# Low-rank rows taken out of the values' products, query copies behind the exponentials, and a moved start of the finishing work

## The chip, the cores and the metric

The kernel runs on one core of one Trainium2 chip. The metric is device time in microseconds for one launch; before the change, three runs took 1050.96, 1053.4 and 1054.88 us, median 1053.4. Times in the trace come from one further, profiled execution.

The engines are named as in the profile: PE multiplies matrices (PEld is its weight load, which overlaps), DVE, ACT and POOL work on vectors, SP only issues DMAs. Each engine runs its own instructions strictly in the order in which they were written, and waits at semaphores for the others. Work is accumulated in PSUM and copied from there to SBUF by ACT and DVE.

## The reference

All is in float32. The batch has 8 sequences of 256 rows of 1,024 features.

```
h    = x @ W.T + b + 2 * (x @ A[slot]) @ B[slot]     # rank 16, one slot per sequence
q, k, v = h @ w_q, h @ w_k, h @ w_v                  # 32 heads, 8 key/value heads, 32 wide
o    = softmax(q k^T / sqrt(32)) v                   # 4 query heads share a k/v head
x1   = x + o @ w_o
c    = x1 @ weight[id].T                             # one 1024x1024 matrix per sequence
out  = x1 + sum_e gate_e(c) * 4 * (c @ A_e.T) @ B_e.T   # 4 experts of rank 16, top 2 by a router
```

The kernel never forms h. It multiplies W and w_q, w_k, w_v once (the fold), so that q, k and v are x times folded weights plus a rank-16 part: u = 2 x A, then u times B folded in the same way. The rank-16 part of all of q, k and v uses the same u. The expert rows A_e and the router's rows are likewise multiplied into each sequence's matrix ("conditioned rows", 68 of them).

Each product of two float32 matrices is made from three products of rounded parts: high x high, high x low, low x high. So a value on its way to PE is first copied as its high part (mostly by ACT), then its low part is the difference (mostly by DVE).

## The kernel before

**Fold stage.** 192 tiles of folded weights are made in three rounds of 4 column blocks (`CHUNKS`), 8 tiles each. Between rounds ACT and DVE copy the folded bias-like rows (`bp`, `brow`), and split the next round's weights (`split_q`, 8 pieces a round).

**Attend stage.** The sequences go in 4 pairs; a pair has 8 key/value heads x 2 sequences = 16 steps (`STEPS`), together N = 64. In step n PE does, in this order (`step` in `tensor`, L838): scores of step n for the maxima, first two of four tiles (L801); work part 0; the outputs of step n-3 (L825, L829); the transposition ("turn") of step n-1's maxima (L836); transposed scores of step n-2, two of four (L812); the other two score tiles of step n; work part 1; the last two transposed scores of n-2. ACT makes the exponentials of the transposed scores (L600), DVE the maxima (L673) and their split into high and low (L679, L681), POOL sums the exponentials (L550), SP sends the maxima to the rows of `q_stack` where they are subtracted by the matmul itself.

**Work** is the projections. The table `WORK` lists for each of a pair's 16 steps what its two parts hold: a unit such as q5 (128 columns of queries for 2 sequences, 24 matmuls of 512 columns and one of the rank-16 part) may be cut, q5:0-3 are the first 3 of its 8 k-steps. A "+" is a unit of the next pair. `SEQ` is the order of units. Unit `u` (L740, L742) makes the rank-16 rows u for both sequences, from the hi and lo parts of A in `a_stack`; v0 to v3 (L774, L776) make the values of 128 tokens each, with 256 columns. The unit's result lies in one of two PSUM banks (`bank`), in turn: the first matmul of a unit waits (`free`, L719) until the unit two before it has been read by ACT (`proj_act`) and by DVE (`proj_dve`).

**Who reads a unit when** is set by `evacuated` (L321): ACT copies units of part 0 before the second pair of exponentials of the same step, those of part 1 behind all exponentials. For q and k, ACT makes 4 copies (L566) and DVE takes 4 differences (L653), then SP issues a DMA that doubles the high part (L479) and PE may use it only then. The next pair's x lands in 8 pieces, ACT copies its high parts (L428: 6 pieces at the end of step 11, 2 at the end of 12), DVE its low parts (L432: steps 12 and 13).

**Finish stage.** Per sequence: `load_o` brings the attention's outputs and the reciprocals of the sums (5 DMAs, L946), `normalise` multiplies them (L1013, DVE), `scale_hi` and `scale_lo` split them; 8 output tiles with w_o (L1043, 24 matmuls of 256 columns each), added to x (`residual`); 8 conditioned rows (L1071), for which POOL loads a 512 KB piece each and ACT and DVE split it (L1052, L1056); then the experts. Part of it is placed in the last pair's steps, whose table of work has holes where a next pair's units would be: `WO_LOAD`, `WO_SPLIT`, `FIRST_TILES` (the 8 output tiles of the first sequence, the first in part 1 of step 12 behind q7, the last in part 0 of step 16), `ROWS_SPLIT` and `ROWS_MULT` (splits and matmuls of the first conditioned rows). Steps are counted from the last pair's start. Rows 5 to 7 come in `first()`, behind the attend stage.

## Time and profile before

| | |
|---|---|
| median of 3 runs (range) | 1053.4 us (1050.96 to 1054.88) |
| the profiled execution | 1050.6 us, of which the span of the trace is 1048.9 us |
| PE busy | 1013.4 us, 97% of the span, 6,934 matmuls |
| weight loads busy | 820.2 us, 78% |
| DVE busy | 633.5 us, 60% |
| ACT busy | 449.5 us, 43% |
| POOL busy | 234.0 us, 22% |
| chain of waits that ended last | PE 90%, DMA 3%, DVE 3% |
| DMA | 117.4 MB, mean 112 GB/s |
| granted TensorE clock, mean | 0.988 of full speed |

"Busy" is the time in which an engine executes; a busy PE may still run at the lower clock. The chain of waits goes back from the last instruction, at each step to what released it. The rows on which the prediction rests stand in a section of their own below; "[1.06 <-PE psS L801]" behind a row of a timeline means that the engine stood idle for so long ahead of it, and what ended that.

### The profile page before, as it was taken

To read this page: it belongs to the slowest core of one execution; us is meant where nothing else is said; L and a number is where in the kernel's file an instruction comes from. 1 tells how busy PE (TensorE), PEld (TensorE's weight loads), DVE (VectorE), ACT (ScalarE), POOL (GpSimd) and SP (SyncE) were. 2 spreads that over 40 slices of the span, in tenths; PEclk is the share of its full clock that TensorE was granted. 3 is DMA by queue.
4 is the path that set the end of the run, shared out by engine and by line. 5 is a ranking of instruction groups with operands and counts; after the bars stand their busy time and mean duration, and the time that the engine had idled before them with its cause. 6 is when DMAs were issued, how large, how long until landed. Compare 5 with 4: busy or idle time off the path is not lost.

```text
span 1048.9 us, 17421 instructions
## 1 busy us (share of the span) xinstructions
PE 1013.4 (97%) x6934; PEld 820.2 (78%) x6934; DVE 633.5 (60%) x1071; ACT 449.5 (43%) x782; POOL 234.0 (22%) x224
## 2 busy tenths in 40 slices
PE   7999999999999999999999999999899999999997
PEld 6878787877678776787767787676589998988986
DVE  6562724667856578664776657654665655655653
ACT  5121223355754557554665556635422332323321
POOL 1000001123323233223332246643111111111100
PEclk9999999999999999999999999999999999999998
DMA  7030312111421124211232134453966756766531
GB/s 263 0 101 1 131 47 73 27 38 43 123 55 38 29 56 122 60 40 27 53 113 60 42 93 142 123 154 142 257 215 197 229 193 199 228 196 205 201 122 40
DMA packets 49888, 117.41 MB, mean 112 GB/s; under 512 B 7298, under 2 KB 26114, under 8 KB 45712
## 3 DMA queue, kind: packets, MB, share of 16 engines
q1 hardware_dynamic: 40080, 81.70, 26.4%
q0 software_dynamic: 9728, 34.61, 10.4%
q8 instruction: 55, 0.90, 0.4%
q14 instruction: 25, 0.20, 0.1%
HBM read 86.38 MB, written 18.89 MB: 100 GB/s over the span
## 4 chain that ended last, share of the span: by engine, by line
PE 90%; DMA 3%; DVE 3%; ACT 1%; SPq 1%; issue 1%; POOL 0%; ACTq 0%
PE psP L759 20%; PE psW L1043 17%; PE psF L254 11%; PE psG L1071 8%; PE psO L825 6%; PE psT L812 5%; PE psS L801 5%; PE psP L774 4%; PE psX L1286 3%; PE psO L829 2%; PE psY L1305 2%; PE psF L265 1%; DMA x_raw<-in_xT 1%; PE psM L836 1%; PE psP L740 1%; PE psP L742 1%
## 5 line engine op out<-in xcount | busy, mean ns | idle before, releaser
L673 DVE TENSOR_REDUCE nmax<-psS 128x2 f32<-128x512 f32 x256 | 164.5, 684 | 153.8 <-PE psS L801 152.1
L550 POOL TENSOR_TENSOR p_sum<-probs 128x512 f32<-128x512 f32 x128 | 167.6, 1310 | 372.6 <-ACT probs L600 372.3
L759 PE MATMUL psP<-x_hl,wq 128*128 128x512 f32 x960 | 235.1, 392 | 0.6 <-DVE q_stack L653 0.6
L759 PEld LDWEIGHTS psP<-x_hl,wq 128*128 128x128 f32 x960 | 175.2, 189 | 32.8 <-issue 0.8
L1043 PE MATMUL psW<-wq 128*128 128x256 f32 x1536 | 196.7, 283 | 1.6 <-DVE q_stack L653 1.2
L1043 PEld LDWEIGHTS psW<-wq 128*128 128x128 f32 x1536 | 190.3, 191 | 6.2 <-issue 1.3
L600 ACT ACTIVATE probs<-psT 128x512 f32<-128x512 f32 x256 | 139.2, 596 | 54.4 <-PE psT L812 53.9
L1052 ACT ACTIVATE cond_hi<-cond_raw 128x1024 fp32r<-128x1024 f32 x64 | 66.8, 1057 | 152.5 <-PE psG L1071 148.1
L1056 DVE TENSOR_TENSOR cond_lo<-cond_raw,cond_hi 128x1024 fp32r<-128x1024 f32 x64 | 78.3, 1235 | 89.1 <-ACT cond_hi L1052 89.0
L812 PE MATMUL psT<-q_stack,k_stack 98*128 98x512 f32 x256 | 90.1, 427 | 7.7 <-ACT probs L600 5.4
L653 DVE TENSOR_TENSOR q_stack<-psP,q_stack 32x512 fp32r<-32x512 f32 x128 | 87.8, 686 | 9.2 <-ACT q_stack L566 7.1
L801 PEld LDWEIGHTS psS<-k_stack,q_stack 96*128 96x128 f32 x512 | 80.0, 190 | 12.7 <-DVE nmax L673 1.1
L615 ACT ACTIVATE nmax_rows<-psM 16x128 f32<-16x128 f32 x64 | 17.1, 267 | 169.6 <-PE psM L836 169.6
L1003 POOL DMA_DIRECT2D cond_raw<-in_cond x64 | 33.8, 529 | 250.0 <-PE psG L1071 249.9
L801 PE MATMUL psS<-k_stack,q_stack 96*128 96x256 f32 x512 | 85.3, 287 | 0.1
L566 ACT ACTIVATE q_stack<-psP 32x512 fp32r<-32x512 f32 x128 | 75.2, 587 | 9.7 <-PE psP L766 8.1
L254 PE MATMUL psF<-q_hi,w_hi 128*128 128x512 f32 x184 | 72.0, 391 | 2.6 <-DVE bp L217 2.6
L254 PE MATMUL psF<-q_lo,w_hi 128*128 128x512 f32 x184 | 71.7, 389 | 0.0
L254 PE MATMUL psF<-q_hi,w_lo 128*128 128x512 f32 x184 | 71.6, 389 | 0.0
L825 PE MATMUL psO<-probs,v_sb 128*32 128x256 f32 x1024 | 69.3, 388 | 0.0
L812 PEld LDWEIGHTS psT<-q_stack,k_stack 98*128 98x128 f32 x256 | 43.0, 191 | 17.1 <-ACT probs L600 10.7
L825 PEld LDWEIGHTS psO<-probs,v_sb 128*32 128x32 f32 x1024 | 26.9, 110 | 31.5 <-issue 18.1
(122 smaller groups left out, 1252.8 us busy)
## 6 DMA issues: line engine op xcount, KB each, us to landing
cond_raw<-in_cond POOLq DMA_DIRECT2D x64, 512.0 KB, 4.1
x_raw<-in_xT SPq DMA_DIRECT2D x32, 256.0 KB, 3.9
q_stack<-q_stack SPq DMA_DIRECT2D x32, 256.0 KB, 3.1
o_scratch<-o_sb SPq DMA_DIRECT2D x64, 128.0 KB
o_raw<-rden_scratch SPq DMA_DIRECT2D x32, 256.0 KB, 5.4
o_raw<-o_scratch SPq DMA_DIRECT2D x8, 1024.0 KB, 8.8
...
outT<-x_sb SPq DMA_DIRECT2D x32, 256.0 KB, 2.5
```

Of the source, the lines that this page charges most:

```text
L254: mm = pe.matmul(psF[:, bank(j, m)], w[:, k, m * P:(m + 1) * P], q[:, k], start=(k == 0 and i == 0), stop=(k == KT - 1 and i == 2))
L550: pool.tensor_tensor(p_sum[:, heads], probs[:, 0, heads], probs[:, 1, heads], ALU.add).then_inc(sum_done, 1)
L600: nc.scalar.activation(probs[:, i % 2, (i // 2) * 512:(i // 2 + 1) * 512], psT[:, i % 2], ACT.Exp, scale=ATT_SCALE).then_inc(exp_done, 1)
L653: ins = dve.tensor_tensor(to(h), both(psP[32 * h:32 * h + 32, bank(p, u)]), f(hi(h)), ALU.subtract)
L673: dve.tensor_reduce(nmax[:, n % 2, 2 * hp:2 * hp + 2, qt], psS[:, i % 2].rearrange("p (h k) -> p h k", h=2), AX.X, ALU.max, negate=True).t ...
L759: mm = pe.matmul(out, wq[:, i, w, k * P:(k + 1) * P], x[:, k, part], start=(k == 0 and n_ == 0), stop=False)
L801: mm = pe.matmul(psS[:, i % 2, j * T:(j + 1) * T], q_stack[0:96, slot, c, 2 * hp + j, qt * P:(qt + 1) * P], k_stack[0:96, c, g], start=Tru ...
L812: pe.matmul(psT[:, kt], k_stack[0:98, c, g, kt * P:(kt + 1) * P], q_stack[0:98, slot, c, 2 * hp:2 * hp + 2].rearrange("p h t -> p (h t)"), ...
L825: pe.matmul(psO[HD * h:HD * h + HD, 0], v_sb[:, c, kt, g], probs[:, kt, h * T:(h + 1) * T], start=(kt == 0), stop=(kt == KK - 1))
L1043: mm = pe.matmul(out, wq[:, k, w, m * P:(m + 1) * P], o_part(n % 2, o)[:, k], start=(k == 0 and i == 0), stop=(k == KT - 1 and i == 2))
L1056: dve.tensor_tensor(cond_lo[:, r % RAW], cond_raw[:, r % RAW], f(cond_hi[:, r % SPLIT]), ALU.subtract).then_inc(cond_lo_done, 1)
L1071: mm = pe.matmul(psG[0:EC, half], a[:, k], w[:, half * 512:(half + 1) * 512], start=(k == 0 and i == 0), stop=(k == KT - 1 and i == 2))
```

## The change

1. Unit `u` and `a_stack` go. The low-rank factor A is put beside the folded weights of the values, in `v_hi`, so that the values' matmuls give 288, 272 and 256 columns instead of three times 256, and the additional columns are x A for the unit's 128 tokens. DVE sums its two parts (`u_tok`), a new unit `t` turns it by 4 PE transposes, and ACT and DVE write `u_stack`.
2. Values get their rank-16 part in two units of their own, r0 and r1 (2 matmuls each), which DVE adds to `v_sb`; `v_sb` exists twice, for alternate pairs.
3. The order of units is new (`SEQ`, `WORK`): v0 to v3, t, k0, q0, q1 of the next pair in the steps 13 to 15.
4. `evacuated` is replaced by `soon` (values, t, q0) and `late` (other q and k): their copies stand behind all exponentials of the step.
5. The splits of x are spread over steps 11, 12 and 13. In the fold stage `bp` and `brow` are copied behind 2 of the 8 splits.
6. The last pair: q7 ends in step 11; `load_o(0)` is issued at the end of step -1 (the step before the last pair's first), `normalise(0)` at the end of step 0; 7 output tiles come in steps 12 to 15, the eighth in `first()` between rows 5 and 6; conditioned rows start at step 16; splits of rows are spread; the second sequence's outputs are loaded and normalised in steps 13 to 16.

```diff
-    (["+u:0-4"], ["+u:4-8"]),
-    (["+k0"], ["+q0"]),
-    (["+q1:0-4"], ["+q1:4-8"]),
+    (["+v0:0-4", "+v1:0-4"], ["+v0:4-8", "+v1:4-8"]),
+    (["+v2", "+v3"], ["+t", "+k0"]),
+    (["+q0"], ["+q1"]),
...
-SEQ = ["u", "k0", "q0", "q1", "v0", "q2", "v1", "v2", "v3", "q3", "k1", "q4", "q5", "q6", "q7"]
...
+SEQ = ["v0", "v1", "v2", "v3", "t", "k0", "q0", "q1", "q2", "r0", "r1", "q3", "k1", "q4", "q5", "q6", "q7"]
...
-def evacuated(n, part):
-
-    if part:
-        return finished(n, 1)
-    late = [(p, u) for p, u in finished(n - 1, 0) if u == "v0"] if n else []
-    return late + [(p, u) for p, u in finished(n, 0) if u != "v0"]
...
+def soon(n, part):
+
+    return [(p, u) for p, u in finished(n, part) if u[0] not in "qk" or u == "q0"]
...
+def late(n):
+
+    return [v for part in range(2) for v in finished(n, part) if v not in soon(n, part)]
...
-            ins = nc.scalar.activation(a_stack[:, c, :, c * R:(c + 1) * R], a_raw[:, c], ACT.Copy)
+            ins = nc.scalar.activation(v_hi[:, :, factor(c, 0)], a_raw[:, c], ACT.Copy)
...
-            for unit_ in evacuated(n, 1):
+            for unit_ in late(n):
...
+        def copy_t(p):
+
+            act.wait_ge(proj_done, unit(p, "t") + 1)
+            nc.scalar.activation(u_stack[0:32], psP[0:32, bank(p, "t")], ACT.Copy, scale=LORA_SCALE)
+            nc.scalar.activation(u_stack[32:64], psP[0:32, bank(p, "t")], ACT.Copy, scale=LORA_SCALE).then_inc(proj_act, 1)
...
+            if p >= 2:
+                act.wait_ge(pv_done, STEPS * (p - 1))
+            nc.scalar.activation(v_sb[p % 2][:, c, t % 2],
+                                 psP[:, bank(p, f"v{t}"), c * V0:c * V0 + NKV].rearrange("p (g d) -> p g d", g=G),
                                  ACT.Copy).then_inc(proj_act, 1)
...
-            for unit_ in evacuated(n, 0):
+            for unit_ in soon(n, 0) + soon(n, 1):
...
+            if more and s == 12:
+                for k in range(3, 6):
+                    split_x_hi(act, p + 1, k)
...
-            if more:
-                for k in {11: range(0, 6), 12: range(6, KT)}.get(s, ()):
+            if more and s == 11:
+                for k in range(3):
                     split_x_hi(act, p + 1, k)
-            for unit_ in evacuated(n, 1):
-                if unit_[1][0] != "v":
-                    evacuate(*unit_)
+            for unit_ in late(n):
+                evacuate(*unit_)
...
+            if more and s == 12:
+                for k in range(6, KT):
+                    split_x_hi(act, p + 1, k)
...
+            if u[0] == "v":
+
+                c, rows = j // 2, NKV * (1 - j // 2)
+                dve.wait_ge(proj_done, unit(p, u) + 1)
+                if p and j == 0:
+                    dve.wait_ge(proj_done, unit(p - 1, "t") + 1)
+                dve.tensor_reduce(u_tok[:, j, c], psP[:, bank(p, u), rows:rows + 2 * R].rearrange("p (h r) -> p r h", h=2),
...
+            elif u[0] == "r":
+                values = v_sb[p % 2][:, j].rearrange("p k g d -> p (k g d)")
+                dve.wait_ge(proj_done, unit(p, u) + 1)
+                dve.wait_ge(proj_act, read_unit(p, f"v{2 * j + 1}") + 1)
+                dve.tensor_tensor(values, values, psP[:, bank(p, u)], ALU.add).then_inc(r_added, 1)
...
-                for k in {12: range(0, 6), 13: range(6, KT)}.get(s, ()):
+                for k in {12: range(3), 13: range(3, 6)}.get(s, ()):
                     split_x_lo(dve, p + 1, k)
-            for unit_ in evacuated(n - 1, 1) if n else [(0, "q1")]:
-                if unit_[1] != "u":
+            for unit_ in late(n - 1) if n else [(0, "q1")]:
+                evacuate(*unit_)
+            if more and s == 13:
+                for k in range(6, KT):
+                    split_x_lo(dve, p + 1, k)
+            for unit_ in soon(n, 0):
+                if unit_[1] != "q0":
                     evacuate(*unit_)
             ahead.vector(dve, n, 0)
...
                 q, v = i // NS, SEQ[i % NS]
-                if v in SEQ_DVE:
-                    pe.wait_ge(proj_dve, dve_unit(q, v) + 1)
+                if v[0] == "r":
+                    pe.wait_ge(r_added, 2 * q + int(v[1]) + 1)
+                else:
+                    pe.wait_ge(proj_act, read_unit(q, v) + 1)
+                    pe.wait_ge(proj_dve, read_unit(q, v) + 1)
...
+        def turn_rows(p):
+            free(p, "t")
+            pe.wait_ge(proj_dve, read_unit(p, "v3") + 1)
+            for t in range(TILES):
+                mm = pe.transpose(psP[0:32, bank(p, "t"), t * P:(t + 1) * P],
+                                  u_tok[:, t].rearrange("p c r -> p (c r)"), id_sb[:])
+            mm.then_inc(proj_done, 1)
...
+        def project_v(p, t, first, end):
+
+            c, toks = t // 2, slice(t * P, (t + 1) * P)
+            if first == 0:
+                free(p, f"v{t}")
+                if t == 0:
+                    pe.wait_ge(a_lo_done, p + 1)
+            out = psP[:, bank(p, f"v{t}")]
+            hi_rows, lo_rows, lo_out = ((slice(V0, VC), slice(V0, VC - R), slice(0, NKV + R)) if c == 0 else
+                                        (slice(0, VC - V0), slice(R, VC - V0), slice(R, NKV + V0)))
+            for k in range(first, end):
+                if t == 0:
+                    pe.wait_ge(x_lo_done, KT * p + k + 1)
+                pe.matmul(out[:, 0:NKV + V0], x[:, k, 0, toks], v_hi[:, k, hi_rows], start=(k == 0), stop=False,
+                          skip_group_check=True)
+                pe.matmul(out[:, lo_out], x[:, k, 1, toks], v_hi[:, k, lo_rows], start=False, stop=False,
...
+                mm = pe.matmul(out[:, c * V0:c * V0 + NKV], x[:, k, 0, toks], v_lo[:, k], start=False, stop=(k == KT - 1),
...
+        def low_rank_v(p, c):
+            free(p, f"r{c}")
+            for t in range(2):
+                toks = slice(c * T + t * P, c * T + (t + 1) * P)
+                mm = pe.matmul(psP[:, bank(p, f"r{c}"), t * NKV:(t + 1) * NKV], u_stack[:, toks],
+                               b_stack[:, VB * P:(VB + 2) * P], start=True, stop=True)
+            mm.then_inc(proj_done, 1)
...
+    ROWS_HI = {14: [0], 15: [1], 16: [2, 3], 17: [4], 18: [5]}
+    ROWS_LO = {(15, 0): [0], (15, 1): [1], (16, 1): [2, 3], (17, 1): [4], (18, 1): [5]}
+    ROWS_MULT = {(16, 0): 0, (16, 1): 1, (17, 1): 2, (18, 0): 3, (18, 1): 4}
+    ROWS_LOAD = {13: range(4), 16: range(4, 6)}
...
-    FIRST_TILES = {(12 + (m + 1) // 2, (m + 1) % 2): m for m in range(KT)}
+    FIRST_TILES = {place: m for m, place in enumerate([(12, 0), (12, 1), (13, 0), (13, 1), (14, 0), (14, 1), (15, 0)])}
...
+        if s == -1:
+
+            sp.wait_ge(before.proj_done, unit(PAIRS - 1, "v3") + 1)
...
         if s == 13:
+            load_o(sp, 1)
             load_x(sp, 1)
-            load_o(sp, 1)
...
-        if s == 10:
+        if s == 1:
             scale_hi(act, 0)
...
+        if s == 15:
+            scale_hi(act, 1)
 
...
-        if part == 0 and s == 10:
+        if part == 1 and s == 0:
             normalise(dve, 0)
-        if part == 1 and s == 11:
+        if part == 1 and s == 2:
             scale_lo(dve, 0)
         m = FIRST_TILES.get((s, 0) if part else (s - 1, 1))
...
-        if part == 1:
-            for r in ROWS_SPLIT.get(s, ()):
-                cond_row_lo(dve, r)
+        if part == 1 and s == 14:
+            normalise(dve, 1)
+        for r in ROWS_LO.get((s, part), ()):
+            cond_row_lo(dve, r)
+        if part == 0 and s == 16:
+            scale_lo(dve, 1)
...
             pool.wait_ge(before.proj_done, PAIRS * NS)
-            load_cond(pool, 0, range(RAW))
+        if s in ROWS_LOAD:
+            load_cond(pool, 0, ROWS_LOAD[s])
...
                     cond_row(KT * n + m + 2)
+                if m == 5 and n == 0:
+                    residual(dve, 0, KT - 1)
...
-            for k in (5, 6, 7):
-                cond_row(pe, 0, k)
+            cond_row(pe, 0, 5)
+            w_o_tile(pe, 0, KT - 1, range(KT))
+            cond_row(pe, 0, 6)
+            cond_row(pe, 0, 7)
...
-            if j:
...
+            if j == 1:
+                act.wait_ge(bp_stored, 32)
...
+            if j + 1 < CHUNKS:
+                for k in range(2, KT):
+                    split_q(j + 1, k)
```

**PE at the start of a pair's step 13.** `psP` are the projections' banks. Before, behind the scores:

```order
L801 MATMUL psS<-k_stack,q_stack 128x256 [waits s_max]
L801 MATMUL psS<-k_stack,q_stack 128x256
L740 MATMUL psP<-x_hl,a_stack 64x256 [waits a_lo_done,x_lo_done,proj_dve,proj_act]
L742 MATMUL psP<-x_hl,a_stack 32x256
L740 MATMUL psP<-x_hl,a_stack 64x256
L742 MATMUL psP<-x_hl,a_stack 32x256
L740 MATMUL psP<-x_hl,a_stack 64x256 [waits x_lo_done]
```

In the change, at the same place; the third row from the end is the first matmul of v1, whose bank was q7's:

```order
L835 MATMUL psP<-v_hi,x_hl 128x272
L837 MATMUL psP<-v_lo,x_hl 128x256
L833 MATMUL psP<-v_hi,x_hl 128x288 [waits x_lo_done]
L835 MATMUL psP<-v_hi,x_hl 128x272
L837 MATMUL psP<-v_lo,x_hl 128x256
L833 MATMUL psP<-v_hi,x_hl 128x288 [waits x_lo_done]
L835 MATMUL psP<-v_hi,x_hl 128x272
L837 MATMUL psP<-v_lo,x_hl 128x256
L833 MATMUL psP<-v_hi,x_hl 128x288 [waits proj_dve,proj_act]
L835 MATMUL psP<-v_hi,x_hl 128x272
L837 MATMUL psP<-v_lo,x_hl 128x256
```

The 32 narrow matmuls of `u` are gone, and two units of the values are started in one part of the step, so a second wait for `proj_dve` and `proj_act`, that of the unit two before v1, now stands 12 matmuls behind the first.

**ACT in the steps 11 and 12 of a pair.** L428 and L566 of before are L471 and L606 of the change: pieces of the next pair's x, and the query copies. Before, from x piece 5 on:

```order
L428 ACTIVATE x_hl<-x_raw 128x512 [waits x_landed5]
L615 ACTIVATE nmax_rows<-psM 16x128 [waits turned]
L600 ACTIVATE probs<-psT 128x512 [waits pv_done,st_done]
L600 ACTIVATE probs<-psT 128x512 [waits st_done]
L608 ACTIVATE o_sb_83<-psO 128x512 [waits o_stored1,pv_done]
L566 ACTIVATE q_stack<-psP 32x2x256 [waits proj_done,st_done]
L566 ACTIVATE q_stack<-psP 32x2x256 x3
L600 ACTIVATE probs<-psT 128x512 [waits st_done] x2
L428 ACTIVATE x_hl<-x_raw 128x512 [waits x_landed6]
```

In the change, from x piece 2 on:

```order
L471 ACTIVATE x_hl<-x_raw 128x512 [waits x_landed2]
L656 ACTIVATE nmax_rows<-psM 16x128 [waits turned]
L641 ACTIVATE probs<-psT 128x512 [waits pv_done,st_done]
L641 ACTIVATE probs<-psT 128x512 [waits st_done]
L649 ACTIVATE o_sb_86<-psO 128x512 [waits o_stored1,pv_done]
L471 ACTIVATE x_hl<-x_raw 128x512 [waits x_landed3]
L471 ACTIVATE x_hl<-x_raw 128x512 [waits x_landed4]
L471 ACTIVATE x_hl<-x_raw 128x512 [waits x_landed5]
L641 ACTIVATE probs<-psT 128x512 [waits st_done] x2
L606 ACTIVATE q_stack<-psP 32x2x256 [waits proj_done,st_done]
L606 ACTIVATE q_stack<-psP 32x2x256 x3
```

The query copies (here q7's) have moved from ahead of the last two exponentials to behind them, and three pieces of x from ahead of the turned maxima (`nmax_rows`) to behind the output copy.

**DVE around the first normalisation.** L1013 of before is L1094 of the change; `nmax` are maxima. Before, in step 10 of the last pair:

```order
L679 CAST nmax_parts<-nmax 128x8 [waits s_max]
L681 TENSOR_TENSOR nmax_parts<-nmax,nmax_parts 128x8 [waits nmax_hi]
L673 TENSOR_REDUCE nmax<-psS 128x2 [waits s_done] x2
L1013 TENSOR_TENSOR o_raw<-o_raw 128x2048 [waits o_landed_0]
L673 TENSOR_REDUCE nmax<-psS 128x2 [waits s_done] x2
L679 CAST nmax_parts<-nmax 128x8 [waits s_max]
L681 TENSOR_TENSOR nmax_parts<-nmax,nmax_parts 128x8 [waits nmax_hi]
```

In the change, from step 0 of the last pair to step 1; L717 is the addition of r0 to the values:

```order
L733 CAST nmax_parts<-nmax 128x8 [waits s_max]
L735 TENSOR_TENSOR nmax_parts<-nmax,nmax_parts 128x8 [waits nmax_hi]
L1094 TENSOR_TENSOR o_raw<-o_raw 128x2048 [waits o_landed_0]
L727 TENSOR_REDUCE nmax<-psS 128x2 [waits s_done] x2
L717 TENSOR_TENSOR v_sb_83<-v_sb_83,psP 128x512 [waits proj_act,proj_done]
L727 TENSOR_REDUCE nmax<-psS 128x2 [waits s_done] x2
L733 CAST nmax_parts<-nmax 128x8 [waits s_max]
L735 TENSOR_TENSOR nmax_parts<-nmax,nmax_parts 128x8 [waits nmax_hi]
```

The wait for `o_landed_0` stands ten steps earlier, ahead of step 1's maxima and of r0's addition.

## Rows read from the trace of the kernel before

**Rows 1.** The page's first part: busy us, share of the span, instructions
```profile
PE 1013.4 (97%) x6934; PEld 820.2 (78%) x6934; DVE 633.5 (60%) x1071; ACT 449.5 (43%) x782; POOL 234.0 (22%) x224
```

**Rows 2.** What PE waited for: line and releaser, us, times, longest
```profile
PE psG L1071 <- DVE cond_lo L1056: 6.6, 4, 3.4
PE psT L812 <- ACT probs L600: 5.4, 3, 2.3
...
PE psF L254 <- DVE bp L217: 2.6, 2, 1.4
PE psT L812 <- DMA q_stack<-nmax_rows: 2.3, 1, 2.3
PE psW L1043 <- DVE q_stack L653: 1.2, 1, 1.2
```

**Rows 3.** Timeline, PE, the first pair's low-rank rows: start, length, line, operation, tiles
```profile
162.49 0.33 PE L740 MATMUL psP<-x_hl,a_stack 128*64 128x256 f32 x1
...
166.28 5.64 PE L759 MATMUL psP<-x_hl,wq 128*128 128x512 f32 x24
```

**Rows 4.** Timeline of PE, step 0 of the second pair
```profile
312.59 0.63 PE L801 MATMUL psS<-k_stack,q_stack 96*128 96x256 f32 x4
313.06 3.02 PE L774 MATMUL psP<-wq,x_hl 128*128 128x256 f32 x24
315.92 0.28 PE L776 MATMUL psP<-b_stack,u_stack 98*128 98x256 f32 x1
...
317.57 0.28 PE L836 MATMUL psM<-id_sb,nmax_parts 128*16 128x128 f32 x1
...
318.62 2.91 PE L759 MATMUL psP<-x_hl,wq 128*128 128x512 f32 x12
321.37 0.63 PE L812 MATMUL psT<-q_stack,k_stack 98*128 98x512 f32 x2
```

**Rows 5.** Timeline of ACT, the same step
```profile
312.56 1.09 ACT L600 ACTIVATE probs<-psT 128x512 f32<-128x512 f32 x2 [2.35 <-PE psT L812]
313.53 2.40 ACT L566 ACTIVATE q_stack<-psP 32x512 fp32r<-32x512 f32 x4
...
318.12 1.09 ACT L600 ACTIVATE probs<-psT 128x512 f32<-128x512 f32 x2
319.09 0.60 ACT L608 ACTIVATE o_sb<-psO 128x512 f32<-128x512 f32 x1
```

**Rows 6.** Timeline of DVE, the same step
```profile
318.58 1.29 DVE L673 TENSOR_REDUCE nmax<-psS 128x2 f32<-128x512 f32 x2 [1.06 <-PE psS L801]
...
320.64 0.17 DVE L681 TENSOR_TENSOR nmax_parts<-nmax,nmax_parts 128x8 fp32r<-128x8 f32 x1
```

**Rows 7.** Timeline of SP's DMA issues, the same step
```profile
315.95 0.56 SPq L479 DMA_DIRECT2D q_stack<-q_stack  x1
```

**Rows 8.** The page's sixth part: DMA issues, KB each, median us to landing
```profile
q_stack<-q_stack SPq DMA_DIRECT2D x32, 256.0 KB, 3.1
```

**Rows 9.** Groups of ACT's instructions: busy us, mean ns, idle before, releaser
```profile
L428 ACT ACTIVATE x_hl<-x_raw 128x512 fp32r<-128x512 f32 x32 | 19.8, 635 | 38.7 <-DMA x_raw<-in_xT 38.3
...
L587 ACT ACTIVATE v_sb<-psP 128x256 f32<-128x256 f32 x16 | 6.3, 395 | 8.1 <-PE psP L776 8.1
```

**Rows 10.** Groups of DVE's instructions, the same columns
```profile
L653 DVE TENSOR_TENSOR q_stack<-psP,q_stack 32x512 fp32r<-32x512 f32 x128 | 87.8, 686 | 9.2 <-ACT q_stack L566 7.1
```

**Rows 11.** Timeline of PE, before the second pair's low-rank rows
```profile
278.50 0.98 PE L812 MATMUL psT<-q_stack,k_stack 98*128 98x512 f32 x2 [1.39 <-ACT probs L600]
```

**Rows 12.** Timeline of SP's DMA issues, the first load of attention outputs
```profile
659.62 1.73 SPq L946 DMA_DIRECT2D o_raw<-rden_scratch  x4
```

**Rows 13.** Timeline of DVE, the first normalisation
```profile
669.52 2.29 DVE L1013 TENSOR_TENSOR o_raw<-o_raw 128x2048 f32<-128x2048 f32 x1 [4.35 <-DMA o_raw<-o_scratch]
```

**Rows 14.** Stretches: us, PE, PEld, DVE, ACT, POOL busy, PE clock, DMA share, GB/s
```profile
719.22:757.12 37.90, 30.21 (x218) 19.93 (x217) 20.79 (x28) 20.90 (x27) 10.63 (x13) 0.95 0.57 164
280.60:283.90 3.30, 3.30 (x22) 2.42 (x24) 3.23 (x5) 3.21 (x6) 1.01 (x1) 0.51 0.42 79
```

296 lines of the change are left out of this document (143 added, 153 removed).

## The prediction

> **What bounds the kernel now.** I read the busy shares first: PE is busy for 97% of the span [rows 1], so a matmul that goes comes off the span, and an idle PE is as dear as a matmul. The list of what PE waited for comes next [rows 2]; together it is small, and these entries bear on the change: 6.6 us for conditioned rows, 5.4 us for exponentials in three places, 2.6 us for `bp`, 2.3 us for an `nmax_rows` transfer, 1.2 us for a query's low part. The timelines of PE, ACT and DVE around one step [rows 4 to 6] then give a clock by which I place every moved instruction. Call T the start of a step's first scores (312.59), and "turn" its transposition of the maxima (317.57). Then: work begins at T+0.47; from the end of the first piece of work (about 316.04) to the turn are 1.53 us; the second piece of work begins at turn+1.05 [rows 4]. ACT does two exponentials until turn+1.64 and the output copy until turn+2.12; the exponentials at a step's end reach T+1.06 of the next, and four query copies behind them T+3.34 [rows 5]. DVE starts the second pair of maxima at turn+1.01 and has split them at turn+3.25 [rows 6].
>
> **Matmuls.** A pair's low-rank rows took 32 matmuls in 3.79 us [rows 3]; four pairs, one of them slowed in part by the clock: 14.9 us go. The value products widen from 3 x 256 columns to 288, 272 and 256. 24 of 256 columns take 2.86 us, 119 ns each, and 12 of 512 take 2.75, 229 ns each [rows 4], so 0.43 ns a column: 48 columns x 32 x 4 pairs = 2.6 us. Below, the widening could be free, if it is the weight load that sets the pace at 256 columns; above, if 288 and 272 cost as much as 512, 256 matmuls x 110 ns = 28 us. I take 2.4, next to the 256-column row. Sixteen transposes of 128 columns are new: between 0.03 us (gap behind the turn) and 0.12 us (a 256-column matmul) each, I take 1.2 in all. Low-rank matmuls for the values stay four a pair. Sum -11.3.
>
> **Fold.** `bp` and `brow` are copied behind two splits of queries' weights, not eight; PE's two waits, 2.6 us [rows 2], end, and the six splits moved behind have 11 us until PE wants them (k=2 comes two rounds of 24 matmuls later). -2.6. The first transposition waits for the fourth value unit's reduction, +0.6; a 0.6 us wait for q1 goes. Zero.
>
> **The pair's end, where x is split.** Before, ACT stood on a landing x and the exponentials came late, once in each of three pairs: 1.39 us in the first [rows 11], 5.4 us in all [rows 2]. Three of the splits now stand behind the output copy, so that goes: -5.4. What is late next is `v1`. Its PSUM bank was q7's, and q7 is now read last. ACT in step 12: until turn+2.12 as above, three x splits of 0.635 [rows 9] to 4.0, two exponentials (1.1) to 5.1, four copies (2.4) to 7.5. DVE: split maxima 3.25, two maxima of step 13 to 4.55, three x parts of 0.69 to 6.6, four lows of q7 of 0.686 [rows 10] to 9.35. PE reaches `v0` at turn+2.55, would start `v1` at 4.1, stops at `v0`'s fourth k until 5.2, and then at `v1` until 9.35. That is 5.2 us, in three pairs +15.6. Bounds: 3.4 each if ACT's copies alone counted (7.5), 6.6 if a late x holds ACT by the 1.4 us of before once more. Behind the standing `v1` are the outputs, the turn and the next exponentials, so nothing fills the gap.
> The transposition `t` in step 14 needs v2 copied, which ACT does behind exponentials and output copy: turn+2.12 and a copy of 0.395 [rows 9], 2.5; PE is there at turn+1.05. 1.5 us, three times: +4.5 (0 to 2 each).
>
> **Copies of queries behind exponentials.** They end at T+3.34; the duplicating DMA is issued at once [rows 7] and lands 3.1 us later [rows 8]: T+6.45 of the step after. q5 (needed after step 9 of 4 k-steps, 0.47+2.06+1.53+2.1 = 6.15) 0.3 us x 4; q6 (step 11, nothing in its second part, 6.0) 0.45 us x 3; q0, now finished in the pair's last step: ready at turn+2.12+2.4+3.1 = 7.6, wanted at turn+1.05+5.7+0.47 = 7.2, 0.45 us x 3. Together +4.0 (0 to 9). SP issues the next x loads behind q6's duplicate; x has 6 us of slack there.
>
> **The last pair.** `load_o(0)` moves to the end of step -1 and its normalisation to DVE at the end of step 0. SP issues it behind q1's duplicate: T+3.95. Before, five DMAs of 2.1 MB needed from 659.62 [rows 12] to 669.52, where DVE had waited 4.35 us [rows 13]: 9.9 us. So they land at T+13.9, the product of 2.29 ends at 16.2, the next maximum at 16.9, while PE wants that buffer at T+12.0 (6.9 for the step, 5.1 into the next). Behind DVE's wait stand maxima and r0's sum, for which q3 waits. 4.9 + 0.9 = 5.8 us against 2.3 before [rows 2]: +3.5. Bounds 0 and 9.
> The trace moved these loads at 212 GB/s. The Trainium skill, DMA: Bandwidth & Descriptors, section Specifications, gives some 358 GB/s for a core's share of HBM; by that the loads take 5.9 us, an estimate from the page, the wait shrinks to about 1 us and the whole sum would be some 5 us less. The measured landing decides.
> q7 is read before the first output tiles: -1.2 [rows 2], and 0.5 of small waits.
> Tail: the stretch 719.22 to 757.12 held 37.9 us with PE busy 30.2, in part at half clock [rows 14]. Rows 0 to 4 and their splits come half a step to a step sooner and a 2.9 us tile stands between rows 5 and 6, where the transfers of rows 6 and 7 are awaited. Against that row 0 now waits for the last maxima (about 1.0, behind a 2.29 normalisation on DVE) and the outputs for exponentials that ACT does late (1.6); 0.9 and 0.4 for rows 4 and 5, 2 of small ones: 27.5 of work + 5.9 = 33.4. -4.5 (-8 to +2).
>
> **Clock.** After the 1.39 us wait the granted clock was 0.51 of full, the lower level (1.2 GHz), for 3.3 us [rows 14]; at full load that costs 1.7 us. The waits that go had such stretches, and those that come will have them: three, the one for o, and perhaps one more than before. +1.7 (-5 to +7).
>
> **Sum.** -11.3 - 2.6 - 5.4 + 15.6 + 4.5 + 4.0 + 3.5 - 1.7 - 4.5 + 1.7 = +3.8. The profiled execution took 1050.6 us in all (span 1048.9, 1.7 around it); its like after the change 1054.4. The median of the runs is 2.8 above the profiled one, so 1057.2. I say 1057.
>
> **Rivals.** A, the forecast: new waits eat the matmuls saved, 1049 to 1059. For it: every one of them is an order on a strict queue. Its weakness: they are differences of long sums.
> B, slower by more than 0.5%: the clock. If PE falls to the lower level behind both pieces of the v1 wait and behind `t` as well, three pairs pay 2 x 1.7 more instead of one stretch in all: 6 x 1.7 - 1.7 = 8.5, giving 1065. It decides from a wait of about 1.4 us, which was enough in [rows 11, 14]. With only half of that, 1061. Against it: the rows show one stretch behind one wait, not two within 5 us.
> C, faster: the v1 wait is no longer than what it replaces, because DVE is free when q7's copies come (3.4 us each: 15.6 becomes 10.2), the duplicates land in time (4.0 goes) and so one clock stretch less: 1057 - 5.4 - 4.0 - 1.7 = 1046; with the o loads hidden as well (3.5), 1042. For it: DVE is busy only 60% [rows 1]; against it: not in these steps.
> D, the matmuls saved come through and nothing waits anew: 1053.4 - 11.3 - 2.6 - 5.4 - 4.5 - some of the clock = about 1027. That needs the bank wait of v1 not to be there, and the order of instructions shows it. Inside C's chance, 3 in 100.
> E, the widened products run at the 512-column price: +25, 1082; 2 in 100, inside B.
>
> **How the numbers follow.** A 0.42, B 0.35, C 0.23. Within 0.5% (5.3 us, about what these runs can tell from no change) is 1048.1 to 1058.7: almost all of A. Faster 0.23, same 0.42, slower 0.35. The range of 8 in 10 takes most of B and C: 1041 to 1067; A's own is 1049 to 1059.
>
> **What would show it.** PE busy some 10 us lower, and no `a_stack` matmul. Waits of PE: psP for DVE `q_stack` about 11 us in three places and for `x_hl` about 4; psP for ACT `v_sb` 4.5 us; psS for DMA `q_stack` a few tenths ten times; one stretch of 5 us at the last pair's second step with DVE's normalisation waiting for `o_raw`; `bp` gone. Wrong if the first of these is under 3 us in all (then C), or if the half-clock stretches are eight or more (then B).

## The result and the profile after

The changed kernel takes 1057.3 us (median of 18 runs, 1055.3 to 1060.4), the kernel before on the same chips 1053.5 us (18 runs, 1049.4 to 1057.0). The ratio is 1.0042, 95% interval 1.0028 to 1.0055: slower by 4.4 us by the ratio (the medians themselves are just under 4 us apart). A second measurement of the same file gave 1.0034 (1.0016 to 1.0052). The forecast said 1057, within 0.5% of the kernel before. One execution of c3, of 1403 us, and one of the kernel before beside it, of 2535 us, lie far outside all others and are left out below.

The profiled execution took 1060.4 us (span 1058.5). That is 3.1 us above the median of its kernel, where that of before lay 2.8 us below: the two spans differ by 9.6 us, the kernels by 4.4. What follows places the 9.6 us; the difference to 4.4 is taken up under the clock, below.

The first part of the page of the changed kernel answers to [rows 1]:

```profile
PE 1009.6 (95%) x6822; PEld 813.0 (77%) x6822; DVE 645.9 (61%) x1099; ACT 447.2 (42%) x786; POOL 236.8 (22%) x224
```

PE is busy 3.8 us less and idle 13.4 us more. What it waits for (line, releaser, us in total, times, longest), against [rows 2]:

```profile
PE psP L833 <- DVE q_stack L696: 13.6, 3, 4.5
...
PE psS L878 <- DVE nmax L727: 5.0, 5, 3.2
PE psP L795 <- ACT v_sb L627: 3.7, 3, 1.2
...
PE psP L833 <- DVE x_hl L475: 3.2, 3, 1.1
PE psT L889 <- DMA q_stack<-nmax_rows: 2.2, 1, 2.2
...
PE psG L1152 <- DVE cond_lo L1137: 1.3, 2, 0.9
PE psS L878 <- issue: 1.2, 4, 0.3
PE psO L902 <- ACT probs L641: 0.9, 1, 0.9
...
PE psS L878 <- DMA q_stack<-q_stack: 0.3, 1, 0.3
```

The waits for `bp`, those of the transposed scores for probabilities and most of those for `cond_lo` are gone; 13.6 us for q7's lows in three places are new, with 3.2 us for x. The first of these places in the timeline of PE (L833 and L837 are matmuls of the values, psO the outputs):

```profile
276.89 0.40 PE L833 MATMUL psP<-v_hi,x_hl 128*128 128x288 f32 x1 [1.07 <-DVE x_hl L475]
...
282.07 0.58 PE L833 MATMUL psP<-v_hi,x_hl 128*128 128x288 f32 x1 [4.54 <-DVE q_stack L696]
...
285.06 1.94 PE L902 MATMUL psO<-probs,v_sb 128*32 128x256 f32 x16
...
287.78 0.28 PE L913 MATMUL psM<-id_sb,nmax_parts 128*16 128x128 f32 x1
```

ACT in the same stretch, whose copies of q7 (L606) stand behind the exponentials:

```profile
276.32 2.38 ACT L606 ACTIVATE q_stack<-psP 32x512 fp32r<-32x512 f32 x4
278.61 1.13 ACT L471 ACTIVATE x_hl<-x_raw 128x512 fp32r<-128x512 f32 x2
288.10 0.27 ACT L656 ACTIVATE nmax_rows<-psM 16x128 f32<-16x128 f32 x1 [8.35 <-PE psM L913]
```

DVE in the same stretch, L475 being low parts of x, L696 q7's lows:

```profile
276.15 2.96 DVE L475 TENSOR_TENSOR x_hl<-x_raw,x_hl 128x512 fp32r<-128x512 f32 x3
279.14 2.79 DVE L696 TENSOR_TENSOR q_stack<-psP,q_stack 32x512 fp32r<-32x512 f32 x4
```

DVE makes three low parts of x, then q7's four lows until 281.9; 0.1 us later PE starts v1. Outputs, turn and exponentials follow late and at half clock (16 matmuls of the outputs take 1.94 us), so that ACT stands for 8.35 us.

The last pair's step 1, timeline of PE:

```profile
613.98 0.28 PE L913 MATMUL psM<-id_sb,nmax_parts 128*16 128x128 f32 x1
616.45 0.73 PE L889 MATMUL psT<-q_stack,k_stack 98*128 98x512 f32 x2 [2.20 <-DMA q_stack<-nmax_rows]
620.39 1.40 PE L878 MATMUL psS<-k_stack,q_stack 96*128 96x256 f32 x4 [3.20 <-DVE nmax L727]
621.59 2.93 PE L811 MATMUL psP<-x_hl,wq 128*128 128x512 f32 x6
```

DVE's normalisation (L1094) and the maxima behind it:

```profile
617.44 2.29 DVE L1094 TENSOR_TENSOR o_raw<-o_raw 128x2048 f32<-128x2048 f32 x1 [7.66 <-DMA o_raw<-o_scratch]
619.65 1.28 DVE L727 TENSOR_REDUCE nmax<-psS 128x2 f32<-128x512 f32 x2
```

SP issued the loads at 606.06, and the next maxima's transfer (`nmax_rows`) behind them in its queue:

```profile
606.06 2.01 SPq L1026 DMA_DIRECT2D o_raw<-rden_scratch  x4
...
608.58 1.36 SPq L536 DMA_DIRECT2D q_stack<-nmax_rows  x2
```

The granted clock was at the lower level, 1.2 GHz, in five stretches inside the kernel, as before, but each was 6.8 us long instead of 3.4. A further stretch stands at the very end in both traces, with PE busy 4.5 us in it before and 4.8 after, and is left out here. Windows laid on them in the trace of the changed kernel (us, busy time of PE, PEld, DVE, ACT, POOL, clock, DMA share, GB/s); the last follows no wait of the change:

```profile
280.70:287.50 6.80, 5.42 (x36) 3.77 (x36) 2.51 (x4) 0.00 (x0) 0.00 (x0) 0.52 0.02 5
420.70:427.50 6.80, 5.90 (x38) 3.96 (x39) 2.04 (x4) 0.00 (x0) 0.00 (x0) 0.52 0.00 0
557.20:564.00 6.80, 3.04 (x16) 2.83 (x20) 4.84 (x8) 1.43 (x3) 0.00 (x0) 0.52 0.19 41
618.60:625.40 6.80, 5.01 (x14) 4.08 (x15) 4.47 (x8) 0.42 (x1) 2.25 (x1) 0.52 0.06 21
762.00:768.80 6.80, 6.80 (x30) 5.72 (x30) 3.75 (x22) 1.27 (x2) 0.53 (x1) 0.52 0.80 218
```

The same on the five stretches of the kernel before:

```profile
280.50:283.90 3.40, 3.40 (x23) 2.52 (x24) 3.30 (x6) 3.31 (x6) 1.01 (x1) 0.53 0.41 77
413.70:417.10 3.40, 3.40 (x15) 3.10 (x16) 3.27 (x7) 3.33 (x7) 1.26 (x1) 0.51 0.01 2
550.20:553.60 3.40, 3.40 (x20) 2.59 (x22) 3.30 (x6) 3.34 (x7) 0.89 (x1) 0.52 0.40 77
669.60:673.00 3.40, 3.40 (x12) 2.87 (x11) 3.40 (x3) 3.20 (x6) 2.02 (x1) 0.53 0.00 0
734.50:737.90 3.40, 2.85 (x10) 1.34 (x14) 0.49 (x1) 0.00 (x0) 0.99 (x2) 0.52 0.79 239
```

PE worked 26.2 us at the lower level after the change (5.42 + 5.90 + 3.04 + 5.01 + 6.80) and 16.5 us before; half of the difference, 4.9 us, is its cost, an estimate from these windows.

The same places in both traces, from the timelines of PE, give this table:

| from, to | before | after | difference |
|---|---|---|---|
| start to the first product of the attend stage | 162.5 | 159.0 | -3.5 |
| to the turn in step 12 of the first pair (the x splits) | 113.4 | 112.8 | -0.6 |
| to the same turn of the second pair | 134.4 | 139.5 | +5.1 |
| to the same of the third | 134.5 | 139.4 | +4.9 |
| to the turn in step 2 of the last pair | 58.4 | 78.8 | +20.4 |
| to the turn in step 11 of the last pair | 75.3 | 63.0 | -12.3 |
| to the first transposed conditioned rows | 73.8 | 65.9 | -7.9 |
| to the end | 296.7 | 300.1 | +3.4 |

Much of the last pair's +20.4 and -12.3 is work that was moved: values and conditioned projections come early in the changed order. The middle rows are the plain ones: a whole pair's period is 5 us longer.

### The profile page after: what moved, and what is told of

The parts are those of the page before. It is cut to its first block, busy times and chain, and to the rows that moved or that the text cites. A ratio compares the mean times of both kernels' runs of the same rounds, so it can differ in the third digit from the quotient of the medians.

```text
span 1058.5 us, 17257 instructions
## 1 busy us (share of the span) xinstructions
PE 1009.6 (95%) x6822; PEld 813.0 (77%) x6822; DVE 645.9 (61%) x1099; ACT 447.2 (42%) x786; POOL 236.8 (22%) x224
## 4 chain that ended last, share of the span: by engine, by line
PE 88%; DVE 5%; DMA 3%; ACT 2%; issue 1%; POOL 1%; SPq 0%; ACTq 0%
PE psP L811 19%; PE psW L1124 16%; PE psF L280 12%; PE psG L1152 8%; PE psO L902 6%; PE psS L878 5%; PE psT L889 5%; PE psX L1375 3%; PE psO L906 3%; PE psP L833 2%; PE psY L1394 2%; PE psF L291 2%; DVE nmax L727 2%; PE psP L835 1%; PE psP L837 1%; DVE q_stack L696 1%
## 5 line engine op out<-in xcount | busy, mean ns | idle before, releaser
L592 POOL TENSOR_TENSOR p_sum<-probs 128x512 f32<-128x512 f32 x128 | 171.1, 1338 | 374.7 <-ACT probs L641 374.5
L811 PE MATMUL psP<-x_hl,wq 128*128 128x512 f32 x960 | 240.2, 393 | 0.2 <-DVE v_sb L717 0.2
L1133 ACT ACTIVATE cond_hi<-cond_raw 128x1024 fp32r<-128x1024 f32 x64 | 66.9, 1057 | 151.5 <-PE psG L1152 148.0
L696 DVE TENSOR_TENSOR q_stack<-psP,q_stack 32x512 fp32r<-32x512 f32 x128 | 87.8, 686 | 11.1 <-ACT q_stack L606 9.1
L606 ACT ACTIVATE q_stack<-psP 32x512 fp32r<-32x512 f32 x128 | 75.1, 587 | 8.1 <-PE psP L818 6.6
L833 PE MATMUL psP<-v_hi,x_hl 128*128 128x288 f32 x128 | 40.5, 316 | 16.9 <-DVE q_stack L696 13.6
L902 PEld LDWEIGHTS psO<-probs,v_sb 128*32 128x32 f32 x1024 | 27.1, 111 | 33.0 <-issue 19.3
```

The lines of the kernel that those rows point to most:

```text
L592: pool.tensor_tensor(p_sum[:, heads], probs[:, 0, heads], probs[:, 1, heads], ALU.add).then_inc(sum_done, 1)
L696: ins = dve.tensor_tensor(to(h), both(psP[32 * h:32 * h + 32, bank(p, u)]), f(hi(h)), ALU.subtract)
L811: mm = pe.matmul(out, wq[:, i, w, k * P:(k + 1) * P], x[:, k, part], start=(k == 0 and n_ == 0), stop=False)
L902: pe.matmul(psO[HD * h:HD * h + HD, 0], v_sb[p % 2][:, c, kt, g], probs[:, kt, h * T:(h + 1) * T], start=(kt == 0), stop=(kt == KK - 1))
```

## The experiments

Ratios are to the kernel before in the same session, with 95% intervals; the changed kernel stands at 1.0042 (1.0028 to 1.0055), and one thousandth is 1.05 us.

**e1: v1 behind v0.** In the table of work:

```diff
-    (["+v0:0-4", "+v1:0-4"], ["+v0:4-8", "+v1:4-8"]),
+    (["+v0:0-4"], ["+v0:4-8", "+v1"]),
```

> The changed kernel with one line of its table of work different: step 13 of a pair holds v0:0-4 in part 0 and v0:4-8, v1 in part 1 (in the changed kernel each part holds a half of both). Same instructions, the same order on ACT and DVE. Theory (v1 stands on the bank that q7's lows free last, and nothing behind it could run): by the time part 1 comes the bank is free, PE waits for x pieces instead: about 1.1 us for piece 3 as now, some 2 us for pieces 6 and 7. psP for q_stack falls from 13.6 us in three places to 0, psP for x_hl rises from 3.2 to about 9, and the three stretches of half clock there (6.8 us each) are half as long: 13.6 - 6 + 3 x 1.7 = 12.7 us less, about 1045. Rival (DVE's backlog is what bounds this place, whatever stands first): the wait moves to x_hl in nearly full size, 1055 to 1058.

Measured: 0.9940 (0.9917 to 0.9963), median 1046.5 us, 10.7 us less than the changed kernel by the ratios, and faster than the kernel before. What PE waits for:

```profile
PE psP L833 <- DVE x_hl L475: 9.5, 6, 2.2
```

The 16.8 us for q7's lows and x have become 9.5 us for x alone, and the stretches of low clock at these three places were 3.4 us long in its trace, where they were 6.8. The theory holds: the wait was one of order, not of DVE's total.

**e2: normalisation three steps later.**

```diff
-        if part == 1 and s == 0:
+        if part == 1 and s == 3:
             normalise(dve, 0)
```

and likewise `scale_hi` in step 4, `scale_lo` in step 5.

> The changed kernel with the first sequence's normalisation three steps later (DVE at the end of step 3 of the last pair, its high part on ACT in step 4, its low part in step 5); the loads stay where they are. Theory (DVE stands on the landing loads and the maxima behind it are late): the 3.2 us wait of scores for maxima goes, the 2.2 us for the nmax_rows transfer behind the loads stays, the stretch of half clock there is shorter or the same: 3.2 to 4.9 us less, 1052.5 to 1054. Rival (the loads' transfers, not DVE, hold PE: what it doesn't wait there it waits for the transfers behind them): under 1 us less.

Measured: 0.9987 (0.9961 to 1.0012), 5.8 us less by the ratios, with ends of the two intervals 1.7 and 9.9 us apart. The waits at this place are one chain: in the two traces of the changed kernel PE waits 2.2 or 3.5 us for the `nmax_rows` transfer and 5.0 or 3.3 for `nmax` in all, a sum of 7.2 or 6.8. In e2 it is 3.4 + 2.3 = 5.7, and the low clock behind it lasted 3.4 instead of 6.8 us (1.7 us). So the traces account for 3 us, and the rival (the loads' queue) is right for the first half of the wait. The 1.7 us of clock may be chance: c1 below has the same edit and a wait of 3.5 us here, and 6.8 us of low clock behind it.

**e3: v2 and v3 copied at the start of step 14.**

```diff
+            for unit_ in soon(n, 0):
+                if unit_[1] in ("v2", "v3"):
+                    evacuate(*unit_)
             if 1 <= n <= N:
                 act.wait_ge(turned, n)
```

> The changed kernel with ACT's copies of v2 and v3 (step 14 of a pair) at the start of the step, ahead of the turned maxima, instead of behind two exponentials and the output copy. Theory (the transposition t waits for a bank that ACT reads late): the 3.7 us in three places go but for the 0.4 us of the last reduction, and k0, whose bank is v3's, does not wait either: 3.3 us less, 1054. The clock stretches are elsewhere, so they change nothing. Rival (ACT is late by itself there: what goes is taken by the exponentials that now stand behind the copies): no change, 1057.

Measured: 1.0002 (0.9982 to 1.0023), 4.2 us less; the 3.7 us for `v_sb` are gone from its waits, 0.4 us for `u_tok` stayed. As expected; the profiled execution of e3 also lacks the last stretch of low clock, so the medians and not the two traces give its size.

**e4: query copies ahead of the exponentials.**

```diff
-    return [(p, u) for p, u in finished(n, part) if u[0] not in "qk" or u == "q0"]
+    return [(p, u) for p, u in finished(n, part) if u[0] not in "qk" or part == 0]
```

> The changed kernel with its query and key copies as in the kernel before: a unit finished in part 0 is copied by ACT ahead of the step's last two exponentials, its lows by DVE and its doubling DMA in the same step. PE's order is the changed kernel's. Theory: q7's bank is free some 3 us earlier, but DVE then reaches x piece 3 later (maxima of step 12 and q7's lows stand ahead of it), so v0 waits about 4 us for x_hl in each of three pairs in place of 1.1 + 4.5: 4 to 5 us less with the clock unchanged. The doublings land in time, 1 us less. In all 1051 to 1053. Rival (the copies ahead of exponentials make those late, which is what the change avoids): waits psT or psO for probs of 3 to 6 us come up and the time stays at 1055 to 1059.

Measured: 1.0165 (1.0140 to 1.0190), 13 us slower than the changed kernel. On DVE the lows of these units stand at the end of the same step, as in the kernel before. Both expectations missed, the rival's less. Its waits:

```profile
PE psP L833 <- DVE x_hl L475: 15.0, 3, 5.0
PE psO L902 <- ACT probs L641: 7.8, 8, 1.1
PE psO L906 <- POOL p_sum L592: 6.9, 21, 0.9
```

The place of v1 went the way foreseen, by less: 15.0 us against 13.6 + 3.2, where about 12 were expected. But the outputs now wait 7.8 us for probabilities and 6.9 us, in 21 places, for POOL's sums (0.9 and 1.6 in the changed kernel). One of the 21, in the timeline of ACT:

```profile
226.89 0.60 ACT L649 ACTIVATE o_sb<-psO 128x512 f32<-128x512 f32 x1
227.37 2.40 ACT L606 ACTIVATE k_stack<-psP 32x512 fp32r<-32x512 f32 x4
229.79 1.09 ACT L641 ACTIVATE probs<-psT 128x512 f32<-128x512 f32 x2
```

POOL, adding the probabilities:

```profile
230.96 1.28 POOL L592 TENSOR_TENSOR p_sum<-probs 128x512 f32<-128x512 f32 x1 [2.58 <-ACT probs L641]
```

PE, the outputs:

```profile
230.93 1.07 PE L902 MATMUL psO<-probs,v_sb 128*32 128x256 f32 x16
232.29 0.64 PE L906 MATMUL psO<-p_sum,ones 128*32 128x256 f32 x8 [0.28 <-POOL p_sum L592]
```

Four copies of k1 (2.40 us) stand ahead of the last two exponentials; POOL can sum only at 230.96, and PE's product of the sums waits for it. This is what the copies behind the exponentials avoid.

The same place in the kernel before, step 5 of the second pair, has the copies ahead of the exponentials too, and PE does not wait. PE and POOL:

```profile
361.29 0.28 PE L836 MATMUL psM<-id_sb,nmax_parts 128*16 128x128 f32 x1
...
367.48 1.07 PE L825 MATMUL psO<-probs,v_sb 128*32 128x256 f32 x16
368.37 0.61 PE L829 MATMUL psO<-p_sum,ones 128*32 128x256 f32 x8
```

```profile
366.87 1.29 POOL L550 TENSOR_TENSOR p_sum<-probs 128x512 f32<-128x512 f32 x1 [2.58 <-ACT probs L600]
```

POOL's sum is ready 0.2 us before PE takes it. From the turn to the outputs are 6.2 us there and 5.6 in e4, because the old table puts 6 k-steps between them and the new one 5. It is the same at k1, q5 and q6 (steps 5, 8 and 10) of the other pairs: some 0.2 us to spare in the kernel before (1.1 us once, where PE itself is late), and a wait of 0.28 us in e4. The larger part of e4's new waits, 1.1 us at a time for probabilities, stands at q2 and q3 (steps 1 and 3). The old table ends q2 in a part 1 and has 8 k-steps behind q3, so these places have no like in it.

**b1: the same edit alone in the kernel before.** `evacuated` keeps the values and `u`; q and k go to a list `late`, copied behind the exponentials:

```diff
+def late(n):
+    return [v for part in range(2) for v in finished(n, part) if v[1][0] in "qk"] if n >= 0 else []
```

> The kernel before with one edit of the change alone: query and key copies on ACT behind all exponentials of the step, their lows on DVE in the next step, the doubling DMA at the step's end. Table of work and order of units are the kernel before's, whose parts have holes. Forecast's view (a copy behind the exponentials only makes duplicates and banks late): 0 to 4 us slower. Theory after e4 (the copies ahead of the exponentials make these late, and POOL's sums behind them, but only where the parts of a step are short, as in the change's table): here no change within 2 us, since the kernel before waits for probabilities in three places only, and those behind x. Rival (the edit gains by itself): 4 us or more faster.

Measured: 1.0296 (1.0266 to 1.0327), 31 us slower. The forecast's view had the sign, none had the size. The waits:

```profile
PE psP L763 <- DVE k_stack L660: 13.4, 3, 4.5
PE psT L816 <- ACT probs L608: 10.2, 4, 3.2
...
PE psW L1047 <- DVE q_stack L660: 4.4, 1, 4.4
```

The first of the three for `k_stack` in the timeline of PE:

```profile
304.86 0.63 PE L805 MATMUL psS<-k_stack,q_stack 96*128 96x256 f32 x4
309.94 5.43 PE L763 MATMUL psP<-x_hl,wq 128*128 128x512 f32 x12 [4.45 <-DVE k_stack L660]
```

q1 starts step 15 in k0's bank, which ACT and DVE now read later than q1 would begin: 4.45 us, and half clock behind it (12 matmuls in 5.43 us, against 2.91 in [rows 4]). In the trace there were ten stretches of low clock ahead of the end, five before; PE is busy 14.2 us more and idle 22.7 us more than in the kernel before. So the edit does not fit the old order of units. In the new one q0 is copied soon, and q1, the next user of k0's bank, begins in part 1 of step 15 and not in part 0. For v1, the next user of q7's bank, there is no such room, and there the change pays. That the new order is what the edit needs is read from the tables, no run shows it by itself. Alone the edit costs 31 us, and taking its query copies back within the change costs 13.

**b2: the fold stage's edit alone in the kernel before**, on ACT and DVE:

```diff
-                for k in range(KT):
+                for k in range(2):
                     split_q(j + 1, k)
```

and the splits 2 to 7 behind the copies of `bp` and `brow`.

> The kernel before with the fold stage's edit alone: bp and brow are copied behind two of the eight splits of the next round's query weights instead of all eight. Theory: PE's two waits for bp (2.6 us) go and nothing takes their place, 2.6 us faster. Rival (the six splits behind them are late for the next round, or the wait is only part of the way to the same thing): 0 to 1 us.

Measured: 0.9957 (0.9939 to 0.9976), 4.5 us less (2.5 to 6.4); the theory's 2.6 lies just inside. The wait for `bp` is gone from its trace.

**t1: the eighth output tile ahead**, in part 1 of step 15 instead of between conditioned rows 5 and 6 (`(15, 1)` added to `FIRST_TILES`).

> The changed kernel with the eighth output tile of the first sequence in part 1 of step 15 of the last pair instead of between conditioned rows 5 and 6. Theory (the tile covers the splits of rows 6 and 7, for which PE waits otherwise): 2 to 3 us slower, in waits psG for cond_lo behind the last step, 1.3 us now. Rival (the splits are ready anyway, or the tile fills a wait in step 15 just as well): within 1 us.

Measured: 1.0057 (1.0037 to 1.0076), 1.6 us above the changed kernel with overlapping intervals: not told apart by time. The wait for `cond_lo` rose from 1.3 to 4.2 us, as the theory says.

**c1: e1, e2 and e3 together.**

> The changed kernel with the three edits that each took time off it, together: v1 behind v0 (step 13), the normalisation three steps later, the copies of v2 and v3 at the start of step 14. Theory (three separate waits): their gains add, 9.8 + 3.8 + 4.4 = 18 us less than the changed kernel, a ratio to the kernel before of about 0.987, 1038 to 1040 where that takes 1052. PE then waits some 9 us for x_hl, 3.4 us for nmax_rows, and nothing for v_sb; there are four half-clock stretches at most, of 3.4 us. Rival (part of each gain is the same stretch of clock, counted twice): 1043 to 1046.

Measured: 0.9859 (0.9831 to 0.9887), median 1038.9 us: 19.3 us below the changed kernel. By ratios the three had given 10.7, 5.8 and 4.2, together 20.7. Within the intervals they add.

**c2: the loads apart.** The output's load moves from step -1 to step 0 of the last pair:

```diff
+        if s == 0:
             for i in range(2):
                 sp.wait_ge(before.o_stored[i], 32 * G)
-            load_o(sp, 0)
+            sp.dma_start(o_land(0), oT[0]).then_inc(o_landed[0], 16)
```

> The kernel c1_three with the loads for the first normalisation in two steps of the last pair: the four of reciprocals at the end of step -1, that of the outputs (1 MB) at the end of step 0. Theory (the maxima's transfer stands in the queues behind 2.1 MB): PE's wait for nmax_rows, 3.5 us, goes and with it the half-clock stretch of 6.8 us behind it (3.4 us): 5 to 7 us less than c1_three, ratio to the kernel before about 0.981. Rival (the second load delays the next step's transfer as much): no change.

Measured: 0.9846 (0.9821 to 0.9870), median 1037.5 us. The wait for `nmax_rows` (3.5 us in c1) and the low clock behind it are gone from its trace; the time is 1.4 us below c1, less than expected and not separated from it. The two profiled executions are 6.6 us apart (1045.0 and 1038.3), as expected, but that of c1 was the slowest of its six.

**c3: another order of the splits of x**, on DVE:

```diff
-                for k in {12: range(3), 13: range(3, 6)}.get(s, ()):
+                for k in {12: range(3), 13: range(4, KT)}.get(s, ()):
...
+            if more and s == 12:
+                split_x_lo(dve, p + 1, 3)
             ahead.vector(dve, n, 1)
```

with q7's lows behind parts 4 to 7, and on ACT high parts 6 and 7 ahead of q7's copies.

> The kernel c2_loads_apart with the splits at x reordered: DVE makes x's low part 3 at the end of step 12, parts 4 to 7 at the start of step 13, and q7's lows behind them; ACT makes x's high parts 6 and 7 ahead of q7's copies. Theory (PE asks for x 3 at 1.3 us and for x 6 at 6 us of step 13, for v1's bank at 8 us only): the waits of psP for x_hl, 9.4 us in six places, fall to under 2, those for q_stack stay under 2 in three, and the half-clock stretches there go: 7 to 10 us less, ratio about 0.973, 1023 to 1027 where the kernel before takes 1052. This is the case of the forecast in which nothing waits anew (about 1027). Rival (DVE's queue is full there, the wait only changes its name): 1 to 3 us less.

Measured: 0.9803 (0.9779 to 0.9828), median 1033.6 us, 4.5 us below c2 by the ratios. Between the two expectations:

```profile
PE psP L836 <- DVE q_stack L700: 5.9, 3, 2.0
```

The waits for x are gone, but 2.0 us for q7's lows came back at each pair. Between the turn of step 12 and v1 DVE has two pairs of maxima, their split, five parts of x and four lows to do, and is hardly idle (10.0 us busy of 10.15 in the second pair): here the rival is right in part. The half-clock stretches did not all go either: behind the 2.0 us waits there was one of 3.4 us in two of the three places. c3 beats the kernel before by 2.0% and the changed kernel by 2.4%.

**The control**, the changed kernel once more:

> The changed kernel unaltered, on the chip of these runs, for the size of what the others win. All theories: ratio to the kernel before 1.003 to 1.0055, the three waits for v1's bank 13.6 us.

Measured: 1.0034 (1.0016 to 1.0052), median 1057.3 us, the three waits 13.6 us.

## Why the prediction was right

The time was right to 0.3 us, but two errors of 6 us cancelled. Term by term, from the trace after (waits as PE's list has them, and its busy time):

| term | forecast | measured |
|---|---|---|
| matmuls | -11.3 | -8.7 (busy -3.8, less 4.9 of clock) |
| fold, `bp` | -2.6 | -2.6 (b2 as a whole: -4.5) |
| probabilities behind x | -5.4 | -4.5 (0.9 at the outputs) |
| v1's bank, with x | +15.6 | +16.8 (13.6 + 3.2) |
| transposition `t` | +4.5 | +4.1 (0.4 of it for the last reduction) |
| duplicates of queries | +4.0 | +1.5 at most (0.3 and 1.2 called issue) |
| loads and normalisation | +3.5 | +3.1 (2.2 + 3.2 against 2.3) |
| tail and small waits | -6.2 | -5.1 (`cond_lo` -5.3, the rest in many small ones) |
| clock | +1.7 | +4.9 |
| sum | +3.8 | +9.5 (the executions differ by 9.8) |

The terms together came out 5.7 us too low. The other error is the last step, from the profiled execution to the median. The forecast took the distance of the kernel before, 2.8 us up; for the changed kernel it is 3.1 us down. 1050.6 + 3.8 + 2.8 = 1057.2 and 1050.6 + 9.8 - 3.1 = 1057.3. That the two errors cancelled is luck; the range, 1041 to 1067, would have held either alone.

**v1's bank.** The mechanism, place and size were as forecast: the clock of [rows 4 to 6] put DVE's last low 9.35 us behind step 12's turn and PE at 5.2 us of waiting. Measured were 10.1 us (271.8 to 281.9; the three parts of x took 2.96 us and not 2.07) and 1.07 + 4.54. e1, which changes only where PE asks, took 10.7 us away, and so shows that this wait with the clock behind it was the largest single price of the change.

**The transposition and the normalisation** were right to 0.5 us; e3 confirms the first, e2 the second in sign. In the normalisation the first half of the wait was not DVE's: it was the transfer of maxima behind 2.1 MB in the queue, which the forecast had left out of its chain (it named the next maxima only), and which stood in the same size in the kernel before. The loads landed 11.4 us after their issue (606.06 to 617.44), not 9.9. The estimate by the Trainium skill, DMA: Bandwidth & Descriptors, section Specifications, would have had them land in 5.9 us: this trace is nearly twice that, and the measured landing was the better guide.

**Copies behind the exponentials** is the step of the forecast that was priced wrong. It was costed through its duplicates alone, as +4.0; the doublings were hidden but for some tenths, +1.5 at most. What it buys, shorter waits for probabilities and sums, was not looked at: e4 puts that at 13 us with this table of work, and b1 shows that it can't be had with the old one. Leaving it out did the total no harm, because the forecast started from the kernel before, which waits for probabilities at the three x places only. There a sixth k-step between turn and outputs hides the copies of k1, q5 and q6 with 0.2 us to spare, as the rows under e4 show; the change takes that k-step away and moves the copies, and the two belong together.

**The clock.** The forecast expected one more stretch like that of [rows 14]. There were as many stretches as before, but twice as long: +4.9 and not +1.7. Some 2.0 us of it lie in the last stretch (6.80 us of PE's work in it against 2.85 before), which follows no wait of the change. Rival B had half of the mechanism: behind v1's pair of waits the clock was low for 6.8 us in all three places, behind `t`, where PE waited 1.2 us, in none. On the scale of the profiled execution, where the forecast was 1054.4, B's extra 4 to 8.5 us give 1058.6 to 1062.9, and 1060.4 was measured. In the median it came through less: the mean granted clock was 0.979 or 0.980 in the profiled execution and the others of 1058 to 1060 us, and 0.981 to 0.984 in those of 1055 to 1058 us. The two profiled executions are 0.009 apart (0.988 and 0.979), the medians of all executions with a clock on record 0.006 (0.987 and 0.981). A busy PE loses half of the time at the lower level, so the 0.003 between them is some 3 us, an estimate, and the larger part of the 5.2 us by which the spans (9.6) differ more than the kernels (4.4).

**Rivals.** C (faster, 1046) needed v1's wait at 3.4 us each, the duplicates in time and one stretch of low clock less. Of these the duplicates nearly were in time, the wait was 5.6 us each, and the low clock grew. D, 1027 without new waits, was not a bad number: c3, in which 5.9 us of v1's wait are left, ran in 1033.6. E is out: a unit of the values takes 3.00 us, not 5.6 (24 matmuls from 292.81 to 295.81 in the timeline of PE):

```profile
292.81 0.29 PE L833 MATMUL psP<-v_hi,x_hl 128*128 128x288 f32 x1
...
295.81 0.30 PE L833 MATMUL psP<-v_hi,x_hl 128*128 128x288 f32 x1
```

That is 0.14 us more than the 2.86 us of [rows 4], 2.2 us for 16 units, against 2.4 forecast.

**What stays open.** Why PE's busy time fell by 8.7 us, clock taken out, and not by 11.3. The timelines of PE narrow it. The matmuls that the change touches give 11.3 to 11.8 us, as forecast: the low-rank rows took 3.7 to 3.8 us a pair at full clock, the values' units take 0.14 to 0.17 us more each, the four transpositions 1.5 us in all, the low-rank part of the values 0.6 us less. But the 960 matmuls of queries and keys, the same in number, took 224.6 us and not 222.4, and stand in 116 pieces instead of 91. No run separates the number of pieces from the rest. And t1 leaves the place of the eighth tile undecided within 2 us.
